# Keys and values of a gated attention: one addition for both, the key's bias and the value tiles' fills on GpSimd, tile by tile

## The reference

```python
qkv = (x @ qkv_w + qkv_b).reshape(b, t, 3, H, DH)
...
mem_score = jnp.einsum('bhts,hts->bht', incidence ** 2, weights)
gram_gate = jax.nn.sigmoid(mem_score * mem_scale[None, :, None])[..., None]
kv_geo = (x @ kv_geo_w).reshape(b, t, 2, H, DH)
...
k_enh = k + kv_gate * gram_gate * k_geo
v_enh = v + kv_gate * gram_gate * v_geo
scores = jnp.einsum('bhtd,bhsd->bhts', q, k_enh) * SCALE
```

## Time and profile before

| | before |
|---|---|
| median of 3 runs | 1112.66 us |
| profiled execution, first to last instruction | 1103.5 us |
| the rest (median less that span) | 9.2 us |
| TensorE busy, share of the span | 964.7 us, 87% |
| VectorE | 762.6 us, 69% |
| ScalarE | 592.7 us, 54% |
| GpSimd | 330.1 us, 30% |
| mean granted TensorE clock | 0.927 of full |
| `geometry` in the span | from some 620 to 724 us |
| its loop over key and value tiles | 697.5 to 724 us |

### The profile page before, as it was taken

One profiled execution on the slowest core, in us unless ns is written; L12 is line 12 of the kernel. 1 busy time (PEld: TensorE's weight loads), 2 busy tenths in 40 slices (PEclk: granted clock), 3 DMA queues, 4 the chain that ended last, 5 costly groups with the idle time before them and its releaser, 6 DMA issues. The chain is left out here.

```text
span 1103.5 us, 18648 instructions
## 1 busy us (share of the span) xinstructions
PE 964.7 (87%) x6220; PEld 628.0 (57%) x6220; DVE 762.6 (69%) x2263; ACT 592.7 (54%) x1165; POOL 330.1 (30%) x417
## 2 busy tenths in 40 slices
PE   6889999999999999999749388689999999997474
PEld 4767666767766776677539344344444444444463
DVE  6767758676677767577623699887888888862523
ACT  4866757666676766567312192315555555564120
POOL 2522122211321111122144209143544344521523
PEclk9999999999999999999759598878999999998577
DMA  6440000000000000000250100000000000000623
GB/s 201 110 125 2 1 1 1 1 1 1 1 1 1 1 1 1 1 2 1 83 168 29 48 1 0 1 1 1 1 2 1 1 2 1 1 1 1 206 59 100
DMA packets 49546, 32.16 MB, mean 29 GB/s; under 512 B 9339, under 2 KB 46124, under 8 KB 49452
## 3 DMA queue, kind: packets, MB, share of 16 engines
q1 hardware_dynamic: 47404, 26.72, 8.7%
q0 software_dynamic: 2048, 4.26, 1.2%
HBM read 21.38 MB, written 11.69 MB: 30 GB/s over the span
## 5 line engine op out<-in xcount | busy, mean ns | idle before, releaser
L562 ACT ACTIVATE attn_a_prob<-attn_a_score,attn_a_m_all 128x128 f32<-128x128 f32 (+7 forms) x256 | 188.8, 740 | 50.9 <-DVE attn_a_m_all L482 47.0
L912 ACT ACTIVATE attn_b_probT<-attn_b_st 128x1024 f32<-128x1024 f32 (+1 forms) x192 | 145.2, 808 | 129.5 <-PE attn_b_st L778 128.2
L478 DVE TENSOR_REDUCE attn_a_m_far<-attn_a_score 128x1 f32<-128x512 f32 (+3 forms) x192 | 105.6, 550 | 78.5 <-PE attn_a_score L390 76.3
L402 PE MATMUL attn_a_slot<-tab,attn_a_prob 128*128 128x128 f32 x1152 | 148.8, 273 | 1.4 <-ACT attn_a_prob L562 1.2
L402 PEld LDWEIGHTS attn_a_slot<-tab,attn_a_prob 128*128 128x128 f32 x1152 | 131.7, 140 | 9.9 <-issue 2.1
L414 PE MATMUL attn_a_o<-attn_a_ptsa,Vd 128*64 128x512 f32 x288 | 136.4, 603 | 0.0
L414 PE MATMUL attn_a_o<-attn_a_ptsb,Vd 128*64 128x512 f32 x288 | 136.4, 603 | 0.0
L841 DVE CUSTOM_DVE_ANT_0 attn_b_slot<-attn_b_slot,later 128x128 f32<-128x128 f32 (+3 forms) x256 | 118.5, 521 | 17.8 <-PE attn_b_slot L753 17.8
L571 ACT ACTIVATE attn_a_ptsa<-attn_a_slot 128x512 f32<-128x512 f32 x144 | 85.8, 596 | 80.6 <-PE attn_a_slot L402 80.0
L753 PE MATMUL attn_b_slot<-KS,attn_b_alone 128*128 128x512 f32 (+2 forms) x384 | 123.8, 417 | 4.1 <-POOL attn_b_alone L934 2.5
L482 DVE CUSTOM_DVE_ANT_0 attn_a_score<-attn_a_score,bias_near,attn_a_m_far 128x256 f32<-128x256 f32 (+2 forms) x192 | 107.4, 559 | 6.8
(11 more groups left out here) (244 smaller groups left out, 1855.8 us busy)
## 6 DMA issues: line engine op xcount, KB each, us to landing
moe_weights_w<-in_L_ffn_w_dram SPq DMA_DIRECT2D x32, 256.0 KB, 5.2
to_experts<-xn SPq DMA_DIRECT2D x2, 1056.0 KB, 11.9
moe_experts_xe<-to_experts SPq DMA_DIRECT2D x16, 132.0 KB, 2.9
bias_by_query_and_key<-bias_by_distance SPq DMA_DIRECT2D x2, 1024.0 KB
bias_near<-bias_by_query_and_key SPq DMA_DIRECT2D x2, 1024.0 KB, 6.4
from_experts<-xn SPq DMA_DIRECT2D x2, 1024.0 KB, 11.7
moe_experts_back<-from_experts SPq DMA_DIRECT2D x8, 256.0 KB, 3.8
X<-in_L_attn_a_x_dram SPq DMA_DIRECT2D x2, 512.0 KB, 4.7
```

The source lines that it names most:

```text
L402: ins = nc.tensor.transpose(dst[:, jj * P:(jj + 1) * P], probs(g)[:, 2 * jj + half, i * P:(i + 1) * P], ident[:, :])
L478: nc.vector.tensor_reduce(least, score[t % 2][:, at:at + nk - win], AX.X, ALU.min).then_inc(far_done, 1)
L562: nc.scalar.activation(probs(g)[:, j, 0:nk], score[t % 2][:, at:at + nk], ACT.Exp, bias=m_all[:, j:j + 1], scale=-1.0, accum_out=rowsum[g ...
L912: nc.scalar.activation(probT[n % 2][:, two, lo:], st[:, two, lo:], ACT.Exp, scale=-1.0).then_inc(exp_done, 1)
```

## The change

Three buffers for the keys move out of L_room into the front of `room`, with a stride of 32 numbers per head, as V9 has it; V9 moves behind them. So one access pattern of two halves can cover the key buffer and the value tile, and one VectorE addition with 256 elements per partition writes both (it takes the place of L1831 and of the additions of L1825 and L1833). The key's bias is no longer added by VectorE: GpSimd adds it in place once `kv_read` of the tile has risen, raises `keyed`, and then fills that tile's columns of ones; its wait for all transposed products is gone, and no memset runs ahead of the loop. The VectorE loop becomes `gated_geo(i)`, `low(i - 3)`, `add_geo(i - 1)`. TensorE's and ScalarE's lists are as before.

```diff
+KEYS_HELD = 3
+KEY_ROOM = KEYS_HELD * B_HEADS * 32
 def value_blocks(room):
-    return room[:, 0:TILES * B_HEADS * 32].rearrange(...)
+    return room[:, KEY_ROOM:KEY_ROOM + TILES * B_HEADS * 32].rearrange(...)
...
-        key = [L_room[:, (2 * NK + i) * D:(2 * NK + i + 1) * D].rearrange("p (h d) -> p h d", h=H) for i in range(NK)]
+        key = [room[:, 0:KEY_ROOM].rearrange("p (n h d) -> p n h d", n=NK, h=H)[:, i, :, 0:B_DH] for i in range(NK)]
...
+        def key_and_value(i):
+            k, v = key[i % NK], V9[:, i, :, 0:B_DH]
+            return bass.AP(tensor=k.tensor, offset=k.offset, ap=[k.ap[0], [v.offset - k.offset, 2], k.ap[1], k.ap[2]])
...
             read_scale(1)
-            pool.wait_ge(turned, len(order))
             for i in range(TILES):
+                pool.wait_ge(kv_read, i + 1)
+                nc.gpsimd.tensor_tensor(key[i % NK], key[i % NK], k_bias[:, :].rearrange("p (h d) -> p h d", h=H), ALU.add).then_inc(keyed, 1)
                 nc.gpsimd.memset(V9[:, i, :, B_DH:], 1.0)
...
                                         gate[:, i, :].unsqueeze(1).unsqueeze(3).to_broadcast([P, 2, H, B_DH]), ALU.mult).then_inc(gated, 1)
+            def add_geo(i):
+                dve.wait_ge(gated, i + 1)
                 if i >= NK:
                     dve.wait_ge(rep_done, i - NK + 1)
-                nc.vector.tensor_tensor(key[i % NK][:, :, :], kv_ps[i % NK][:, 0, :, :],
-                                        k_bias[:, :].rearrange("p (h d) -> p h d", h=H), ALU.add).then_inc(based, 1)
-            def add_geo(i):
-                dve.wait_ge(gated, i + 1)
-                nc.vector.tensor_tensor(V9[:, i, :, 0:B_DH], kv_ps[i % NK][:, 1, :, :], geo[i % NK][:, 1, :, :], ALU.add).then_inc(kv_read, 1)
-                dve.wait_ge(based, i + 1)
-                nc.vector.tensor_tensor(key[i % NK][:, :, :], key[i % NK][:, :, :], geo[i % NK][:, 0, :, :], ALU.add).then_inc(keyed, 1)
+                nc.vector.tensor_tensor(key_and_value(i), kv_ps[i % NK][:, 0:2, :, :], geo[i % NK][:, :, :, :], ALU.add).then_inc(kv_read, 1)
...
-            for i in range(1, TILES + 2):
+            for i in range(1, TILES + 3):
                 if i < TILES:
                     gated_geo(i)
+                if i >= 3:
+                    low(i - 3)
                 if i <= TILES:
                     add_geo(i - 1)
-                if i >= 2:
-                    low(i - 2)
```

More of the change, by code:

```diff
@@ L1365, in _ @@
                 ins.then_inc(updated, 1)
+KEYS_HELD = 3
+KEY_ROOM = KEYS_HELD * B_HEADS * 32
 def value_blocks(room):
-    return room[:, 0:TILES * B_HEADS * 32].rearrange("p (t h d) -> p t h d", t=TILES, h=B_HEADS)
+    return room[:, KEY_ROOM:KEY_ROOM + TILES * B_HEADS * 32].rearrange("p (t h d) -> p t h d", t=TILES, h=B_HEADS)
 def geometry(nc, X, stats, xn, xnT, w_geo, sel, decay_logits, scale_row, kv_gate, gate, ident, constants, w_q, q_bias, q_scale, QS4,
@@ L1411, in geometry @@
         zeroed, shifted, q_done, q_ready = ph.sem("zeroed"), ph.sem("shifted"), ph.sem("q_done"), ph.sem("q_ready")
-        NG, NK = H // GRP, 3
+        NG, NK = H // GRP, KEYS_HELD
         geo = [L_room[:, i * 2 * D:(i + 1) * 2 * D].rearrange("p (w h d) -> p w h d", w=2, h=H) for i in range(NK)]
-        key = [L_room[:, (2 * NK + i) * D:(2 * NK + i + 1) * D].rearrange("p (h d) -> p h d", h=H) for i in range(NK)]
+        key = [room[:, 0:KEY_ROOM].rearrange("p (n h d) -> p n h d", n=NK, h=H)[:, i, :, 0:B_DH] for i in range(NK)]
         rep = [L_room[:, 3 * NK * D + i * BANK:3 * NK * D + (i + 1) * BANK].rearrange("p (g a r d) -> p g a r d", g=NG, a=GRP, r=REP)
@@ L1419, in geometry @@
         k_ps = [bank[NK + i] for i in range(NK)]
-        kv_done, gated, based, keyed, kv_read = (ph.sem(n) for n in ("kv_done", "gated", "based", "keyed", "kv_read"))
+        kv_done, gated, keyed, kv_read = (ph.sem(n) for n in ("kv_done", "gated", "keyed", "kv_read"))
         high_done, rep_done, k_done, k_moved = (ph.sem(n) for n in ("high_done", "rep_done", "k_done", "k_moved"))
         widened, rested = ph.sem("widened"), ph.sem("rested")
+        def key_and_value(i):
+            k, v = key[i % NK], V9[:, i, :, 0:B_DH]
+            return bass.AP(tensor=k.tensor, offset=k.offset, ap=[k.ap[0], [v.offset - k.offset, 2], k.ap[1], k.ap[2]])
         def copies(i, r):
```

## The result

The changed kernel takes 1128.30 us (median of 4 runs, 1118.37 to 1130.38) against 1112.62 us before (4 runs, 1111.88 to 1114.72). The ratio is 1.0144 with a 95% interval of 1.0117 to 1.0172: slower by 15.7 us, or 1.4%. The forecast was slower, 1139.3 us, with a range of 1118 to 1143.

What follows compares the result with a forecast made beforehand. The prediction took the loop to become one chain through TensorE and VectorE at half clock: last matmul at 744.3, plus an end of 6.3, gives stage +26.6 us; span 1130.1 plus 9.2 makes 1139.3 us, range 1118 to 1143.

Steps and rivals of the forecast that it cites:

- The stall: Ahead of the loop: without the memsets, the gate's multiplication takes 0.29 instead of 5.13 us and `weigh(1)` starts 4.73 us earlier.
- The ring: Loop: matmul, gating, `low`, transposes, next matmul become one chain, 2.36 us a tile at full clock against 1.48.
- The ring at half clock: Loop: the same chain at half clock takes 4.05 us a tile, against some 2.5 before.
- The clock: TensorE's pause of 3.16 us ahead of the loop drops the clock, which stays at half for the whole loop.
- rival A: Loop: the clock comes back inside it; +14.9 us after half the tiles, +8.1 after two; chance 0.17.
- the +26.6: Stage end: forecast at 750.6 instead of 723.96 us, 26.6 us later, with the whole loop at half clock.
- Rival B: Loop: the clock never falls and tiles take 2.36 us; +3.7 us, time 1116.4; chance 0.10.
- The argument on the clock: Loop: a stretch with PE 85% busy stayed at 0.50, so the new loop, 73% busy, should stay there too.
- The sum against the profiled execution: Whole kernel: span 1103.5 + 26.6 = 1130.1, with the 9.2 us around it 1139.3, taking the profiled execution as the median.
- Rival C: Loop: one tile of distance remains, so VectorE or TensorE sets the pace; -6.0 us, time 1106.7; chance 0.08.
- Rival D: Loop: GpSimd's addition and `low` meet, up to 0.47 us more on each of 12 tiles; time 1144.9; chance 0.03.
- Attention B at half clock from its start: Behind the stage: `attention_b` starts at half clock; nothing taken in the forecast, at most 2 us.

Runs made afterwards that it cites:

- The fills alone: Kernel before, with only GpSimd's fill of each value tile waiting for that tile's `kv_read` instead of all transposed products: 1106.28 us, ratio 0.9964.
- The order experiments: Changed kernel with VectorE's loop as `gated_geo(i)`, `add_geo(i - 1)`, `low(i - 2)`: 1103.08 us; or with `low(i - 3)` ahead of `gated_geo(i)`: 1104.73 us.
- work in the pause: Changed kernel plus three unneeded 128x512 matmuls in TensorE's pause ahead of the loop: 1115.06 us, ratio 1.0041.
- the order of before: Changed kernel with VectorE's loop order of the kernel before, `gated_geo(i)`, `add_geo(i - 1)`, `low(i - 2)`: 1103.08 us, ratio 0.9940.
- the fills undone: Changed kernel with the 16 fills again back to back ahead of the loop, behind the wait for all transposed products: 1128.63 us, ratio 1.0169.

## Why the prediction was right, and where it was not

- *The stall.* 4.73 us were expected, with `key_value(3)` 3.55 us behind the start of the gate's multiplication (693.63 - 690.08); measured 696.78 - 693.18 = 3.60. The fills alone gave 4.8 us of stage. Right.
- *The ring.* The terms at full clock gave 2.36 us, measured 2.36 to 2.37. The order experiments show what made it: with `low` ahead of the wait, and all else as changed, the turn is 1.30 to 1.40. Right, and it decided the sign.
- *The ring at half clock.* Expected 4.05, measured 3.67: the mis-sized term. I took 1.26 us from the transposes' first weight load to the next matmul from the first tile of the earlier trace rows, where the load stood 0.41 us ahead of its matmul; in the steady ring both start at 710.72 and the next matmul at 711.63, 0.91. The rest, 0.03, is in the two steps between the engines. Over ten turns the 0.38 us make 3.8.
- *The clock.* The fall behind a pause of 3.2 us came as expected. "Half clock for the whole loop" did not hold: it rose before the last two turns, 2 x (4.05 - 2.37) = 3.4 us, and left the end at full clock: from the last gating to GpSimd's first instruction of `attention_b` 5.08 us, where I had 6.3 + 0.3. So rival A, the clock coming back inside the loop, was a part of the truth, late in the profiled runs and, to judge by their mean clocks, earlier in the shorter ones (1117 to 1120 us). These three, 3.8 + 3.4 + 1.5 = 8.7, make up, but for rounding and 0.05 us in the first tile, the 8.5 us between the +26.6 and the +18.1 of the stage.
- *Rival B, the clock never falling,* was priced at +3.7 us. The run with work in the pause is that case: stage 38.22 - 34.17 = +4.05, time +4.9. Price right, condition false for the change as made.
- *The argument on the clock* was weak where it went from one stretch, 85% busy, that stayed low to a loop of 73%: in the loop PE was busy 11.60 of 15 us, 77%, and the clock stayed low for 41 us and then rose in the same pattern of work. What decides the moment of the rise stays open; no run here separates it.
- *The sum against the profiled execution.* I added 9.2 us for what lies around the span. The changed kernel's run of 1127.02 has a span of 1124.9, 2.1 apart, and before's later runs lie 1.7 to 3.5 above their spans. The other 7 us would then be this one execution being quicker than the median; its own time is not on record, so that is inferred. It shifted nothing in the forecast difference, but it makes the spans' +21.4 larger than the +15.7 of the medians. Why the medians differ by less than the stages' +18.1 stays open: the first profiled run of the changed kernel is 14.4 us above the before beside it, the second, with the same stage, 18.5. The measured median is inside the range, and one of the eight runs, 1117.28, just below it. The range's upper end, 1143, needs both of the additions that the text joins by "or": 1139.3 + 1.8 + 2; with one of them it is 1141.
- *Rival C, faster,* gave -6.0 us of stage if a tile of distance stays. The kernel with the order of before has just that: 34.17 to 28.16, -6.0, and 7.1 us in time. So its price was right, down to its terms (4.8 for the stall; turns 1.6 us shorter in all, for 1.8; an end 0.4 longer, for 0.6), and its condition false for the change as made.
- *Rival D,* `low` meeting GpSimd's addition: in the changed kernel `low` takes 0.41 to 0.42 us in all turns, and 0.57 once, at the end. In the order of before the GpSimd addition takes 0.56 us instead of 0.45, and starts beside `low` (706.85 against 706.69 to 707.10), so GpSimd is the one held up, by 0.11 us, and it costs nothing, since TensorE has no gap there. Where the addition of GpSimd starts first, 742.41 against 742.57 in the changed kernel, it is `low` that takes 0.57. The hold of 0.11 us is less than the 0.25 us for which `low` still ran. That one holds the other up agrees with the Trainium skill, "SBUF — State Buffer", section "Who interferes with whom" (a VectorE instruction with two SBUF inputs contends with a GpSimd instruction that reads SBUF). The 5.14 against 0.29 us agrees with what the same section says of tensor_scalar.
- *Attention B at half clock from its start,* for which up to 2 us were kept in the range: the case did not arise in the profiled run, since the clock was at 1.00 when `attention_b` began and fell within it, as it did before. From its first GpSimd instruction to the end it took 379.5 us against 379.2.

The version to keep is the changed kernel with the loop `gated_geo(i)`, `add_geo(i - 1)`, `low(i - 2)`: 1103.08 us, faster than the kernel before and the changed kernel. `low` ahead of the gating, 1104.73, can't be told from it.

## What to carry to other kernels

When a step is moved down in one engine's list, write out for every other engine which of its instructions is now ahead of the one that waits for that step. If a tile's consumer on TensorE waits, through VectorE, for TensorE's own last instruction, the overlap is gone, however little work each engine has left. Look at memsets of GpSimd that run ahead of a stage, too: that they are off the path says nothing if a VectorE instruction is held up until the last of them ends, as the 5.13 us one was here.

## What had not been expected of the hardware

The same ring of work ran at half clock for ten turns (PE busy 77%), and at full clock for all its turns (20.39 of 32.00 us, 64%) when the pause of 3.2 us ahead of it was filled. In these profiles the ring kept the level at which it entered for most or, with the fills undone, half of its turns. When the clock rose in it differed: after ten turns in two profiles, after six in one. With that goes a spread of 12 and 16 us between the runs of one kernel, where before's is 4.7. The same fall ahead of the loop cost only 1.9 us with the order of before, where TensorE had no gap behind it and the clock was back after three lengthened turns. So the pause was dear only together with the chain behind it, and filling it in the better kernel brought 1.9 us of stage and no difference in time that the runs could tell.
